# Cross attention on one core: the second score product as two 64-row matmuls instead of two 128-row ones

## The chip, the cores and the metric

The kernel runs on one core of one Trainium2 chip. The metric is device time in microseconds (us). Three runs of the kernel before gave 686.63, 688.91 and 689.27 us; the median is 688.91.

## The reference

For each of 8 batches, with x1 and x2 of shape 512 x 1024 (channels x positions) in float32:

```
q = x1ᵀ Wqᵀ + bq            # 1024 x 64
k = Wk x2 + bk              # 64 x 1024
v = Wv x2 + bv              # 512 x 1024
attn = softmax(q k, axis=2) # 1024 x 1024
out  = v attnᵀ + x1         # 512 x 1024
```

The scores q k contract over 64 rows only. The array of TensorE has 128.

## The kernel before, in words

Every operand of a large product is split into a high part, rounded to the fp32r format, and a low part, the remainder, rounded too. A product is then the sum of three: high·high, high·low, low·high. ScalarE (ACT) makes the high parts by copies, VectorE (DVE) and GpSimd (POOL) make the low parts by subtraction, TensorE (PE) multiplies, and the sync engine (SP) issues all transfers. The order of the work on each engine is written out by hand in one block per engine, and semaphores tie the blocks together.

A batch on PE runs like this (`batch`, L762). The first output half (96 matmuls on `acc_ps`, L731) has the query projection of the next batch (16 matmuls, L670) in its middle. The second output half (96 more) has the key projection of the next batch after its first channel tile and score tiles 0 to 3 of the next batch between its later matmuls. Then `v_phase` (L756) computes the values of the next batch in 8 groups of 12 matmuls (L700), with score tiles 4 to 7 after groups 1, 2, 4 and 5. Seven such batches run in a loop. Batch 0 has a prologue with its own order and the last batch has no successor.

A score tile `scores(t)` (L674) takes 128 queries against all 1024 keys. It fills two banks of `s_ps`, one for each half of the keys, with 512 columns each. Before the change the 128 rows of the stationary operand `q_st` hold the queries' high part in rows 0 to 63 and their low part in rows 64 to 127. The moving operands are `k_hh`, the keys' high part, written twice, once in each half of the partitions, and `k_ll`, the keys' low part, also twice. So a tile is four matmuls of 128 rows and 512 columns: for each key half one with `k_hh` and one with `k_ll`.

These operands come about as follows. PE's projection leaves two partial sums in `s_ps`. ACT copies one of them out (`cross`), DVE joins both with the bias into `full` (`q_sum`, `k_sum`). ACT's `q_high` (L320) copies `full` to the upper rows of `q_st`, and DVE's `q_low` (L467) writes the rest to its lower rows. `k_high` copies twice, `k_low` (L475) subtracts twice over all 1024 columns. `full` is shared by queries and keys.

After a score tile DVE takes the negated row maximum (`neg_max`, L490), ACT the exponential (L337) with the row sum, DVE the reciprocal, the scaling and a transpose in blocks of 32 (`turn`, L506). After four tiles SP issues 16 moves (L208) that put the blocks in place as `pt_raw`. ACT copies `pt_raw` to `pt_hi` and DVE or POOL subtract to `pt_lo` (L455, L271), and these are the moving operands of the output. Between its moves for the second half, SP issues the first load of the next batch's x2, and after them the three others (L184). In ACT's order the rounding of x2's second tile stands before the second `pt_hi` of that half.

Of the kernel before, what the change touches and what calls it, by code (L numbers as in the profile page):

```python
# [36 lines left out]
F32R = mybir.dt.float32r  # L37
# [4 lines left out]
B, C, N, D = 8, 512, 1024, 64  # L42
P = 128
# [3 lines left out]
HALVES = 2  # L47
NH = N // HALVES
# [13 lines left out]
def build(nc, x1_d, x2_d, wq_d, bq_d, wk_d, bk_d, wv_d, bv_d, out_d):  # L62
    with ExitStack() as ctx:
        def sb(name, shape, dt):
            return ctx.enter_context(nc.sbuf_tensor(name, shape, dt))

        def psum(name, shape):
            return ctx.enter_context(nc.psum_tensor(name, shape, F32))

        def sem(name):  # L70
            return ctx.enter_context(nc.semaphore(name))
# [10 lines left out]
        pt_lo = sb("pt_lo", [P, MT, NH], F32R)  # L82
        q_st = sb("q_st", [P, N], F32R)
        k_hh = sb("k_hh", [P, N], F32R)
        k_ll = sb("k_ll", [P, N], F32R)
        cross = sb("cross", [D, N], F32)
        full = sb("full", [D, N], F32)
        o_sb = sb("o_sb", [P, OUTS, NH], F32)
# [21 lines left out]
        s_ps = psum("s_ps", [P, 2, 2, NH])  # L110
# [34 lines left out]
        s_qhi = sem("s_qhi")  # L145
        s_qlo = sem("s_qlo")
        s_khi = sem("s_khi")
        s_klo = sem("s_klo")
# [151 lines left out]
        def _(act):  # L300
            def copy(out, in_):
                return nc.scalar.activation(out, in_, ACT.Copy)  # L302
# [17 lines left out]
            def q_high(b):  # L320
                act.wait_ge(s_qsum, b + 1)
                copy(q_st[0:D, :], full[:]).then_inc(s_qhi, 1)

            def k_cross(b):
                act.wait_ge(s_k, b + 1)
                cross_rows(1).then_inc(s_kcross, 1)
# [43 lines left out]
            def batch(b, last):  # L370
# [6 lines left out]
                if not last:  # L377
                    round_x1(nb, 2)
                    round_x1(nb, 3)
                    q_cross(nb)  # L380
                    round_x2(nb, 0)
                    q_high(nb)
# [45 lines left out]
            q_cross(0)  # L428
            v_hi(0, 2)
            q_high(0)  # L430
            v_hi(0, 3)
            exp(0, 0, first=True)
# [20 lines left out]
        def _(dve):  # L453
            def sub(out, a, hi):
                return nc.vector.tensor_tensor(out, a, hi.bitcast(F32), ALU.subtract)  # L455

            def join(bias, slot):

                return nc.vector.scalar_tensor_tensor(
                    out=full[:], in0=s_ps[0:D, slot, :, :].rearrange("p a n -> p (a n)"), scalar=bias[:, 0:1],  # L460
                    in1=cross[:], op0=ALU.add, op1=ALU.add)

            def q_sum(b):
                dve.wait_ge(s_qcross, b + 1)
                join(bias_q, 0).then_inc(s_qsum, 1)

            def q_low(b):  # L467
                dve.wait_ge(s_qhi, b + 1)
                sub(q_st[D:2 * D, :], full[:], q_st[0:D, :]).then_inc(s_qlo, 1)

            def k_sum(b):
                dve.wait_ge(s_kcross, b + 1)
                join(bias_k, 1).then_inc(s_ksum, 1)

            def k_low(b):  # L475
                for half in range(2):
                    dve.wait_ge(s_khi, b * 2 + half + 1)
                    sub(k_ll[half * D:(half + 1) * D, :], full[:], k_hh[0:D, :]).then_inc(s_klo, 1)

            def low_x1(b, k):  # L480
                dve.wait_ge(s_x1hi, b * KT + k + 1)
                sub(xs_lo[:, k, :], stage[:, k, :], xs_hi[:, k, :]).then_inc(s_x1lo_o, 1)

            def low_x2(b, k):
                dve.wait_ge(s_x2hi, b * KT + k + 1)
                return sub(xs_lo[:, k, :], stage[:, k, :], xs_hi[:, k, :])

            def neg_max(b, t):
                dve.wait_ge(s_s, b * ST + t + 1)
                nc.vector.tensor_reduce(negmax[:, t:t + 1], s_ps[:, t % 2, :, :].rearrange("p a n -> p (a n)"),  # L490
                                        AX_X, ALU.max, negate=True).then_inc(s_max, 1)

            def normalise(b, t):
                dve.wait_ge(s_exp, b * ST + t + 1)
                nc.vector.reciprocal(inv[:, t:t + 1], rowsum[:, t:t + 1]).then_inc(s_inv, 1)
                dve.wait_ge(s_inv, b * ST + t + 1)
                nc.vector.tensor_scalar(probs[:, t % 2, :], probs[:, t % 2, :], inv[:, t:t + 1], None,  # L497
                                        ALU.mult).then_inc(s_norm, 1)

            def turn(b, t, first=False):  # L500

                h, i = t // NT, t % NT
                if i == 0 and not first:
                    dve.wait_ge(s_moved, half_of(b, h) * MOVED - MOVED)
                dve.wait_ge(s_norm, b * ST + t + 1)
                nc.vector.transpose(blocks[:, :, i, :],  # L506
                                    probs[:, t % 2, :].rearrange("p (j r) -> p j r", r=Q)).then_inc(s_blk, 1)

            def v_lo(b, m):
                dve.wait_ge(s_vhi, b * MT + m + 1)  # L510
                sub(vt_lo[:, m, :], acc_ps[:, m % BANKS, :], vt_hi[:, m, :]).then_inc(s_acc, 1)

            def p_lo(b, h, j):

                dve.wait_ge(s_phi, half_of(b, h) * PAIRS + j + 1)
                sub(pt_lo[:, 2 * j:2 * j + 2, :], pt_raw[:, 2 * j:2 * j + 2, :],
                    pt_hi[:, 2 * j:2 * j + 2, :]).then_inc(s_plo, 1)

            def out(b, h, c):

                dve.wait_ge(s_o, b * OG + h * CT + c + 1)
                dve.wait_ge(s_res[c], half_of(b, h) * 16 + 16)
                nc.vector.scalar_tensor_tensor(  # L523
                    out=o_sb[:, c, :], in0=acc_ps[:, c % BANKS, :], scalar=bias_v[:, c:c + 1],
                    in1=o_sb[:, c, :], op0=ALU.add, op1=ALU.add).then_inc(s_acc, 1)
# [23 lines left out]
            def batch(b, last):  # L549
                nb = b + 1  # L550

                dve.wait_ge(s_plo_odd, b * 2 + 2)
                turn(b, 7)
                if not last:
                    low_x1(nb, 1)
                    low_x1(nb, 3)
                out(b, 0, 0)
                out(b, 0, 1)
                if not last:
                    dve.wait_ge(s_klo, nb * 2)  # L560
                    q_sum(nb)
                    q_low(nb)
                out(b, 0, 2)
                for j in range(PAIRS - 1):
                    p_lo(b, 1, j)
                p_lo(b, 1, PAIRS - 1)
                if not last:
                    low_x2(nb, KT - 1).then_inc(s_x2lo_last, 1)
                out(b, 0, 3)

                out(b, 1, 0)
                if not last:
                    dve.wait_ge(s_qlo, nb + 1)
                    k_sum(nb)
                    k_low(nb)
                out(b, 1, 1)
                if last:
                    out(b, 1, 2)
                    out(b, 1, 3)
                    return  # L580
                neg_max(nb, 0)
                normalise(nb, 0)
                neg_max(nb, 1)
                turn(nb, 0)
                out(b, 1, 2)
                normalise(nb, 1)
                neg_max(nb, 2)
                turn(nb, 1)
                normalise(nb, 2)
                neg_max(nb, 3)  # L590
                turn(nb, 2)
                out(b, 1, 3)
                normalise(nb, 3)
                turn(nb, 3)

                v_lo(nb, 0)
                v_phase(nb)
# [25 lines left out]
            q_sum(0)  # L623
            v_lo(0, 2)
            q_low(0)
            v_lo(0, 3)
            neg_max(0, 0)
# [27 lines left out]
            with dve.Fori(0, B - 1) as b:  # L655
                batch(b, False)
# [4 lines left out]
        def _(pe):  # L661
# [10 lines left out]
                return mm  # L672

            def scores(t):  # L674
                rows = q_st[:, t * P:(t + 1) * P]
                for h in range(HALVES):
                    cols = slice(h * NH, (h + 1) * NH)
                    nc.tensor.matmul(s_ps[:, t % 2, h, :], rows, k_hh[:, cols], start=True, stop=False)  # L678
                    mm = nc.tensor.matmul(s_ps[:, t % 2, h, :], rows, k_ll[:, cols], start=False, stop=True)  # L679
                mm.then_inc(s_s, 1)  # L680

            def scores_first(b, t):

                if t == 0:
                    pe.wait_ge(s_qsum, b + 1)
                    pe.wait_ge(s_qlo, b + 1)
                    pe.wait_ge(s_klo, b * 2 + 2)
                else:
                    pe.wait_ge(s_ksum, b + 1)
                scores(t)  # L690
# [185 lines left out]
```

## Time and profile before

| | |
|---|---|
| median of three runs | 688.91 us |
| span of the profiled execution | 687.4 us |
| PE busy | 656.8 us, 96% |
| PE weight loads busy | 534.1 us, 78% |
| DVE busy | 475.1 us, 69% |
| ACT busy | 280.7 us, 41% |
| POOL busy | 139.3 us, 20% |
| matmuls | 2848, of them 256 for the scores |

The profiled execution is known by its span, from its first to its last instruction; a time of its own around the span is not given. Times in the rows are us from the start of the span. A matmul's record lasts longer than the distance to the next matmul's start, because matmuls are pipelined and their ends are modelled. PEld is the weight load that comes before each matmul.

### The profile page before, as it was taken

The page shows a single profiled execution, that of the slowest core. Times are in us where ns is not written, and L with a number is a line of the kernel's source. Part 1 is how long each engine was busy: PE and PEld are TensorE (multiplying, and loading weights), DVE is VectorE, ACT ScalarE, POOL GpSimd, SP SyncE. Part 2 cuts the span into 40 slices and gives each one's busy share as a digit, 9 for nine tenths or more (in the row PEclk, how much of TensorE's full clock was granted, in tenths as well). Part 3 has the DMA queues.
Part 4 walks back from the last instruction along what each step waited for, and adds up shares of the span by engine and source line. Part 5 has one row for each costly group of instructions (what it writes and reads, how often), then busy time and mean ns, then how long its engine had stood idle before and what let it go on. Part 6 is the DMA issues. An engine that isn't in the chain of part 4 may idle for free.

```text
span 687.4 us, 8392 instructions
## 1 busy us (share of the span) xinstructions
PE 656.8 (96%) x2848; PEld 534.1 (78%) x2848; DVE 475.1 (69%) x503; ACT 280.7 (41%) x367; POOL 139.3 (20%) x58
## 2 busy tenths in 40 slices
PE   5999889999999989999899998999989999899997
PEld 3877668887788868888688886888868888788886
DVE  4889558695686765876758866679567695686641
ACT  5564422355235352354423633337232364234220
POOL 0302210063001440032400433005130063101200
PEclk9999989999999999999999999999999999999999
DMA  8400932749328482285624675255941749326351
GB/s 317 187 1 12 265 108 61 193 137 243 102 86 232 116 234 91 84 237 124 197 92 123 197 170 190 75 139 158 229 153 61 174 142 248 107 80 149 73 179 56
DMA packets 94874, 100.04 MB, mean 146 GB/s; under 512 B 8336, under 2 KB 69776, under 8 KB 94864
## 3 DMA queue, kind: packets, MB, share of 16 engines
q1 hardware_dynamic: 94864, 99.91, 51.1%
q8 instruction: 6, 0.10, 0.1%
q14 instruction: 4, 0.03, 0.0%
HBM read 51.64 MB, written 16.78 MB: 100 GB/s over the span
## 4 chain that ended last, share of the span: by engine, by line
PE 81%; DVE 6%; issue 4%; SPq 3%; ACT 3%; DMA 2%; DVEq 0%; ACTq 0%
PE acc_ps L731 39%; PE acc_ps L700 25%; PE s_ps L670 8%; PE s_ps L678 4%; PE s_ps L679 4%; DVE pt_lo L455 4%; SPq L208 3%; DMA stage<-in_ctx_dram 2%; ACT pt_hi L302 2%; ACT xs_hi L302 1%; DVE probs L497 1%; DVE blocks L506 1%; PE s_ps L794 1%; DVE negmax L490 1%; ACT probs L337 0%
## 5 line engine op out<-in xcount | busy, mean ns | idle before, releaser
L731 PE MATMUL acc_ps<-pt_hi,vt_hi 128*128 128x512 f32 x512 | 202.0, 395 | 17.5 <-DVE pt_lo L455 17.5
L731 PE MATMUL acc_ps<-pt_hi,vt_lo 128*128 128x512 f32 x512 | 200.5, 392 | 0.0
L731 PE MATMUL acc_ps<-pt_lo,vt_hi 128*128 128x512 f32 x512 | 200.4, 391 | 0.0
L731 PEld LDWEIGHTS acc_ps<-pt_hi,vt_hi 128*128 128x128 f32 x512 | 96.6, 189 | 44.0 <-DVE pt_lo L455 24.1
L337 ACT ACTIVATE probs<-s_ps,negmax 128x1024 f32<-128x1024 f32 x64 | 71.4, 1116 | 128.4 <-DVE negmax L490 128.4
L271 POOL TENSOR_TENSOR xs_lo<-stage,xs_hi 128x1024 fp32r<-128x1024 f32 x35 | 91.1, 2612 | 156.0 <-ACT xs_hi L302 156.0
L731 PEld LDWEIGHTS acc_ps<-pt_hi,vt_lo 128*128 128x128 f32 x512 | 96.7, 189 | 20.4
L731 PEld LDWEIGHTS acc_ps<-pt_lo,vt_hi 128*128 128x128 f32 x512 | 96.8, 189 | 19.8
L271 POOL TENSOR_TENSOR pt_lo<-pt_raw,pt_hi 128x1024 fp32r<-128x1024 f32 x14 | 41.0, 2946 | 327.5 <-ACT pt_hi L302 327.5
L700 PE MATMUL acc_ps<-wv_hi,xs_hi 128*128 128x512 f32 x256 | 99.9, 390 | 0.0
L700 PE MATMUL acc_ps<-wv_hi,xs_lo 128*128 128x512 f32 x256 | 99.7, 389 | 0.0
L700 PE MATMUL acc_ps<-wv_lo,xs_hi 128*128 128x512 f32 x256 | 99.6, 389 | 0.0
L455 DVE TENSOR_TENSOR pt_lo<-pt_raw,pt_hi 128x1024 fp32r<-128x1024 f32 x46 | 81.8, 1801 | 17.7 <-ACT pt_hi L302 17.4
L490 DVE TENSOR_REDUCE negmax<-s_ps 128x1 f32<-128x1024 f32 x64 | 77.6, 1216 | 11.9 <-PE s_ps L679 11.8
L302 ACT ACTIVATE pt_hi<-pt_raw 128x1024 fp32r<-128x1024 f32 x60 | 60.9, 1049 | 56.8 <-DMA pt_raw<-blocks 35.8
L506 DVE STREAM_TRANSPOSE blocks<-probs 128x1024 f32<-128x1024 f32 x60 | 74.3, 1238 | 6.7 <-DMA pt_raw<-blocks 6.1
L523 DVE SCALAR_TENSOR_TENSOR o_sb<-acc_ps,bias_v,o_sb 128x512 f32<-128x512 f32 x64 | 47.2, 739 | 36.2 <-PE acc_ps L731 35.7
L302 ACT ACTIVATE cross<-s_ps 64x1024 f32<-64x1024 f32 x16 | 16.4, 1025 | 131.5 <-PE s_ps L670 131.5
L455 DVE TENSOR_TENSOR vt_lo<-acc_ps,vt_hi 128x512 fp32r<-128x512 f32 x64 | 43.2, 675 | 35.7 <-ACT vt_hi L302 35.7
L302 ACT ACTIVATE xs_hi<-stage 128x1024 fp32r<-128x1024 f32 x60 | 61.6, 1051 | 10.8 <-DMA stage<-in_ctx_dram 10.7
L700 PEld LDWEIGHTS acc_ps<-wv_lo,xs_hi 128*128 128x128 f32 x256 | 48.2, 188 | 10.0
L700 PEld LDWEIGHTS acc_ps<-wv_hi,xs_hi 128*128 128x128 f32 x256 | 48.2, 188 | 10.0
(49 smaller groups left out, 602.4 us busy)
## 6 DMA issues: line engine op xcount, KB each, us to landing
pt_raw<-blocks SPq DMA_DIRECT2D x240, 128.0 KB, 2.4
stage<-in_ctx_dram SPq DMA_DIRECT2D x32, 512.0 KB, 5.3
o_sb<-in_x_dram SPq DMA_DIRECT2D x64, 256.0 KB, 3.3
out_dram<-o_sb SPq DMA_DIRECT2D x64, 256.0 KB, 2.6
stage<-in_x_dram SPq DMA_DIRECT2D x28, 512.0 KB, 5.9
blocks<-in_x_dram SPq DMA_DIRECT2D x4, 512.0 KB, 8.6
pt_raw<-in_L_xattn_Wv_dram SPq DMA_DIRECT2D x4, 256.0 KB, 8.0
pt_raw<-in_L_xattn_Wk_dram SPq DMA_DIRECT2D x1, 128.0 KB, 3.4
```

The source lines that it names most:

```text
L271: return nc.gpsimd.tensor_tensor(out, src, hi.bitcast(F32), ALU.subtract)
L302: return nc.scalar.activation(out, in_, ACT.Copy)
L337: nc.scalar.activation(probs[:, t % 2, :], s_ps[:, t % 2, :, :].rearrange("p a n -> p (a n)"), ACT.Exp, bias=negmax[:, t:t + 1], accum_out ...
L455: return nc.vector.tensor_tensor(out, a, hi.bitcast(F32), ALU.subtract)
L490: nc.vector.tensor_reduce(negmax[:, t:t + 1], s_ps[:, t % 2, :, :].rearrange("p a n -> p (a n)"), AX_X, ALU.max, negate=True).then_inc(s_m ...
L506: nc.vector.transpose(blocks[:, :, i, :], probs[:, t % 2, :].rearrange("p (j r) -> p j r", r=Q)).then_inc(s_blk, 1)
L523: nc.vector.scalar_tensor_tensor(out=o_sb[:, c, :], in0=acc_ps[:, c % BANKS, :], scalar=bias_v[:, c:c + 1], in1=o_sb[:, c, :], op0=ALU.add ...
L670: mm = nc.tensor.matmul(s_ps[:, slot, h, :], weights[:, k, :], cols, start=(k == 0 and part == 0), stop=(k == KT - 1 and part == 1))
L678: nc.tensor.matmul(s_ps[:, t % 2, h, :], rows, k_hh[:, cols], start=True, stop=False)
L679: mm = nc.tensor.matmul(s_ps[:, t % 2, h, :], rows, k_ll[:, cols], start=False, stop=True)
L700: mm = nc.tensor.matmul(acc_ps[:, m % BANKS, :], x[:, k, cols], w[:, k, :], start=(k == 0 and w is wv_hi and x is xs_hi), stop=(k == KT - ...
L731: mm = nc.tensor.matmul(acc_ps[:, c % BANKS, :], v[:, m, cols], p[:, m, :], start=(m == 0 and v is vt_hi and p is pt_hi), stop=(m == MT - ...
```

## The change

In place of `k_ll` there are two buffers. `k_lo` holds the low part of the first key half in partitions 0 to 63 and of the second key half in partitions 64 to 127. `q_dup` holds a second copy of the queries' high part in partitions 64 to 127. A score tile is now two 128-row matmuls with `k_hh` as before, and then two matmuls of 64 rows: `q_st`'s upper rows times the first half of `k_lo` into the first bank, and `q_dup`'s rows times the second half of `k_lo` into the second bank. The product of the two low parts, which the 128-row form added as well, is left out. ACT makes one more copy per batch, DVE subtracts half as many columns, and three waits are added or moved.

```diff
-        k_ll = sb("k_ll", [P, N], F32R)
+        q_dup = sb("q_dup", [P, N], F32R)
+        k_lo = sb("k_lo", [P, NH], F32R)
...
                 copy(q_st[0:D, :], full[:]).then_inc(s_qhi, 1)
+                copy(q_dup[D:2 * D, :], full[:]).then_inc(s_qhi, 1)
...
             def q_low(b):
-                dve.wait_ge(s_qhi, b + 1)
+                dve.wait_ge(s_qhi, b * 2 + 1)
...
             def k_low(b):
-                for half in range(2):
-                    dve.wait_ge(s_khi, b * 2 + half + 1)
-                    sub(k_ll[half * D:(half + 1) * D, :], full[:], k_hh[0:D, :]).then_inc(s_klo, 1)
+                for h in range(HALVES):
+                    dve.wait_ge(s_khi, b * 2 + h + 1)
+                    cols = slice(h * NH, (h + 1) * NH)
+                    sub(k_lo[h * D:(h + 1) * D, :], full[:, cols], k_hh[0:D, cols]).then_inc(s_klo, 1)
...
                     dve.wait_ge(s_qlo, nb + 1)
+                    dve.wait_ge(s_qhi, nb * 2 + 2)
                     k_sum(nb)
...
             def scores(t):
-                rows = q_st[:, t * P:(t + 1) * P]
+                rows = slice(t * P, (t + 1) * P)
                 for h in range(HALVES):
-                    cols = slice(h * NH, (h + 1) * NH)
-                    nc.tensor.matmul(s_ps[:, t % 2, h, :], rows, k_hh[:, cols], start=True, stop=False)
-                    mm = nc.tensor.matmul(s_ps[:, t % 2, h, :], rows, k_ll[:, cols], start=False, stop=True)
+                    nc.tensor.matmul(s_ps[:, t % 2, h, :], q_st[:, rows], k_hh[:, h * NH:(h + 1) * NH],
+                                     start=True, stop=False)
+                for h, q_hi in enumerate((q_st[0:D, rows], q_dup[D:2 * D, rows])):
+                    mm = nc.tensor.matmul(s_ps[:, t % 2, h, :], q_hi, k_lo[h * D:(h + 1) * D, :],
+                                          start=False, stop=True)
                 mm.then_inc(s_s, 1)
...
                     pe.wait_ge(s_qlo, b + 1)
+                    pe.wait_ge(s_qhi, b * 2 + 2)
                     pe.wait_ge(s_klo, b * 2 + 2)
```

## Rows read from the trace of the kernel before

**Rows 1.** The page, part 1: busy us (share of the span) xinstructions.

```profile
PE 656.8 (96%) x2848; PEld 534.1 (78%) x2848; DVE 475.1 (69%) x503; ACT 280.7 (41%) x367; POOL 139.3 (20%) x58
```

**Rows 2.** The page, part 4: the chain that ended last, by engine.

```profile
PE 81%; DVE 6%; issue 4%; SPq 3%; ACT 3%; DMA 2%; DVEq 0%; ACTq 0%
```

**Rows 3.** Windows of two batches: us, busy of each engine, granted clock, DMA.

```profile
core 0: us, PE busy (x) PEld busy (x) DVE busy (x) ACT busy (x) POOL busy (x), PEclk, DMA share, GB/s
...
174.57:258.04 83.47, 80.55 (x352) 65.94 (x353) 58.79 (x63) 34.54 (x45) 18.82 (x7) 1.00 0.54 151
...
340.59:423.12 82.53, 80.52 (x353) 65.92 (x353) 58.87 (x63) 34.44 (x45) 18.89 (x7) 1.00 0.54 153
```

**Rows 4.** Timeline of PE around one score tile: start us, us, engine, line, operation.

```profile
194.45 0.39 PE L678 MATMUL s_ps<-k_hh,q_st 128*128 128x512 f32 x1
...
195.35 0.39 PE L731 MATMUL acc_ps<-pt_hi,vt_hi 128*128 128x512 f32 x1
```

**Rows 5.** Timeline of PE and its weight loads just after a stall.

```profile
174.57 0.19 PEld L731 LDWEIGHTS acc_ps<-pt_hi,vt_hi 128*128 128x128 f32 x1 [2.10 <-DVE pt_lo L455]
174.57 0.50 PE L731 MATMUL acc_ps<-pt_hi,vt_hi 128*128 128x512 f32 x1 [1.67 <-DVE pt_lo L455]
174.68 0.19 PEld L731 LDWEIGHTS acc_ps<-pt_lo,vt_hi 128*128 128x128 f32 x1
...
174.91 0.40 PE L731 MATMUL acc_ps<-pt_lo,vt_hi 128*128 128x512 f32 x1
```

**Rows 6.** Timeline of weight loads in the prologue: eight in a row.

```profile
45.06 0.86 PEld L794 LDWEIGHTS s_ps<-ident,probs 128*128 128x128 f32 x8 [0.45 <-DVE probs L497]
```

**Rows 7.** Groups by line and form: count, busy us, mean ns of one, idle before.

```profile
L679 PE MATMUL s_ps<-k_ll,q_st 128*128 128x512 f32 x128 | 49.9, 390 | 0.0
...
L455 DVE TENSOR_TENSOR k_ll<-full,k_hh 64x1024 fp32r<-64x1024 f32 x16 | 19.5, 1218 | 8.1 <-ACT k_hh L302 7.9
...
L302 ACT ACTIVATE q_st<-full 64x1024 fp32r<-64x1024 f32 x8 | 8.4, 1056 | 2.9 <-DVE full L459 2.9
```

**Rows 8.** Timeline of ACT from the queries' copy to the second output half.

```profile
161.03 1.06 ACT L302 ACTIVATE q_st<-full 64x1024 fp32r<-64x1024 f32 x1 [0.39 <-DVE full L459]
165.51 1.06 ACT L302 ACTIVATE pt_hi<-pt_raw 128x1024 fp32r<-128x1024 f32 x1 [3.41 <-PE acc_ps L731]
```

**Rows 9.** Timeline of ACT and DVE in the prologue.

```profile
29.32 1.06 ACT L302 ACTIVATE q_st<-full 64x1024 fp32r<-64x1024 f32 x1 [0.90 <-DVE full L459]
...
30.55 0.60 ACT L302 ACTIVATE vt_hi<-acc_ps 128x512 fp32r<-128x512 f32 x1 [0.16 <-PE acc_ps L700]
...
32.94 1.23 DVE L490 TENSOR_REDUCE negmax<-s_ps 128x1 f32<-128x1024 f32 x1 [0.58 <-PE s_ps L679]
```

**Rows 10.** Timeline of DVE from the first score tile to the last turn.

```profile
189.66 1.23 DVE L490 TENSOR_REDUCE negmax<-s_ps 128x1 f32<-128x1024 f32 x1 [1.60 <-PE s_ps L679]
...
204.14 1.25 DVE L506 STREAM_TRANSPOSE blocks<-probs 128x1024 f32<-128x1024 f32 x1
...
230.23 0.16 DVE L495 RECIPROCAL inv<-rowsum 128x1 f32<-128x1 f32 x1 [0.37 <-ACT probs L337]
```

**Rows 11.** Timeline of SP's queue: moves and x2 loads.

```profile
205.41 10.53 SPq L208 DMA_DIRECT2D pt_raw<-blocks  x16
...
244.34 1.70 SPq L184 DMA_DIRECT2D stage<-in_ctx_dram  x3
...
327.65 1.74 SPq L184 DMA_DIRECT2D stage<-in_ctx_dram  x3
```

**Rows 12.** Timeline of ACT where it uses moved and loaded data.

```profile
217.89 2.01 ACT L302 ACTIVATE pt_hi<-pt_raw 128x1024 fp32r<-128x1024 f32 x2 [2.56 <-DMA pt_raw<-blocks]
...
250.03 1.06 ACT L302 ACTIVATE xs_hi<-stage 128x1024 fp32r<-128x1024 f32 x1 [0.90 <-DMA stage<-in_ctx_dram]
...
332.50 1.04 ACT L302 ACTIVATE xs_hi<-stage 128x1024 fp32r<-128x1024 f32 x1
```

**Rows 13.** Window of the first loop batch with the lower clock.

```profile
87.40:95.10 7.70, 6.71 (x18) 4.80 (x17) 5.53 (x4) 0.46 (x1) 1.51 (x1) 0.56 0.45 147
```

## The prediction

> **What bounds the kernel now.** I read the profile in this order. First the busy table: PE is busy 96% of the 687.4 us span, DVE 69% [rows 1]. Then the chain of waits: PE holds 81% of it [rows 2]. Then the windows by batch, cut at the point where PE leaves its stall: an undisturbed batch lasts 82.53 us, 80.52 of it PE, so PE idles 2.0 us per batch [rows 3]. All of that idleness sits at the start of the second output half, where PE waits for DVE's pt_lo; elsewhere the loop's matmuls follow each other without a gap. Then the timeline around one score tile: matmul starts at 194.45 and, four later, at 195.35 [rows 4], a pitch of 0.227 us (0.90 / 4). So 8 score tiles of 4 matmuls cost PE 7.3 us per batch, and every one of them stands on PE's own time.
>
> What a weight load costs shows only after a stall [rows 5]. The load starts at 174.57 and its matmul record is 0.50 us long instead of 0.39; the next load starts at 174.68 and the next matmul at 174.91. So a load occupies the array 0.11 us, the next load begins when the matmul before it starts to stream, and it is hidden under the 0.23 us of streaming. Eight loads in a row took 0.86 us [rows 6], again 0.11 each.
>
> **The change on PE.** A score tile was four 128-row matmuls (64 tiles, 256 matmuls, half of them on k_ll [rows 7]). It becomes two 128-row matmuls and then two 64-row ones on different rows of the array and different PSUM banks. The instruction count is the same, so the gain exists only if the last two stream side by side. The trace of before has no 64-row matmul, so I bound the pair's time P against today's 2 x 0.227 = 0.454:
> - Lower bound: both loads (2 x 0.11 = 0.22) hide under the matmul ahead, and both stream together, P = 0.227, a saving of 0.227 per tile.
> - By the order in rows 5, one load ahead at a time: the second load starts when the first 64-row matmul streams, so the second starts 0.11 later, P = 0.34, a saving of 0.117.
> - Serial: P = 0.454, saving 0.
> - Upper bound: going from 128-row to 64-row work and back empties the array. A matmul's record is 0.389 against a pitch of 0.227, so waiting for its end costs 0.162, twice per tile 0.324; if the loads come out from cover too, 2 x 0.11 more. Net 0.10 (with the full saving) to 0.43 dearer per tile.
>
> I take 0.117, because rows 5 are the nearest to it: they show when a load is let go.
>
> Two rules of the Trainium skill pull apart here. "TensorE: Matmul & The Clock Gate", the part on packing small matmuls, says that loads for other row groups are pulled ahead and that packed matmuls start some 4 ns apart: that would be the lower bound, 64 x 0.227 = 14.5 us of PE work. "TensorEngine Tiling (Array Packing)", Key Properties, says that changing the tiling mode, not merely the tile, drains the engine; this kernel changes it twice in each tile, which would be the upper bound. No run so far shows either.
>
> **The change on ACT and DVE.** ACT gains one 64x1024 copy (q_dup) per batch: 1.06 us, as q_st's [rows 7]. In the loop it comes after the copy at 161.03 and before pt_hi at 165.51, ahead of which ACT sits idle 3.41 us [rows 8]: hidden, with 2.3 us to spare. Without that cover it would be 1.06 x 7 = 7 us. DVE's q_low waits for the first copy only. PE's new wait for the second copy comes some 25 us later in the loop. In the prologue it does not hide fully: q_st ends at 30.38, q_dup would end at 31.4, and v_hi (30.55 before), and v_lo on DVE behind it, slip so that the first neg_max (32.94 [rows 9]) starts up to 0.3 us later. k_low goes from 2 x 1.22 to about 2 x 0.65 us (half the columns and a little; my estimate): DVE is 1.1 us less busy, but DVE then waits 1.60 us for PE before neg_max [rows 10], so it gives nothing. The extra DVE wait before k_sum was met long before.
>
> **What is late next.** PE's saving is worth its full size only while the other chain follows. From the first score tile of a batch, DVE and ACT run a chain of their own [rows 10]: neg_max at 189.66, dense work to the turn at 204.14; then 16 moves take SP 10.53 us [rows 11]; ACT waits 2.56 us for them at 217.89 [rows 12]; DVE is dense again and idles only 0.37 before the last reciprocal. Then come 16 moves more, the three x2 loads, the copy xs_hi and behind it pt_hi. These loads have little slack: issued at 327.65, used at 332.50 (4.85 us) in a good batch; issued at 244.34, used only at 250.03 with 0.90 us of waiting in the one bad batch, and that batch lasted 83.47 instead of 82.5 [rows 3, 11, 12]. So per batch the first tile's saving is free, and of the other seven tiles' saving only 0.37 us plus the loads' slack (0 to about 0.8, I take 0.4) gets through.
>
> **Sum.** With 0.117 per tile, the seven tiles bring PE 0.82 us of lead, of which 0.37 + 0.4 = 0.77 count; with the first tile 0.89 us per batch, times 7 batches = 6.2. The prologue's 8 tiles give 0.94 less 0.3 for q_dup, 0.6; but one load in seven that lands late takes some 0.6 back. Total 6.2 us: span 687.4 to 681.2. The span of the profiled execution is 1.5 below the median of the runs (688.91), and what lies around it does not change: 682.7 us. With the lower bound the seven tiles lead by 1.59 and again 0.77 get through: (0.23 + 0.77) x 7 + 1.5 = 8.5 us, 680.4; with the loads' slack at 0.8 it would be 677. With 0.117 and no slack in the loads: (0.117 + 0.37) x 7 + 0.6 = 4.0, 684.9. The answer is thus nearly the same for both ways of overlapping: 677 to 685.
>
> **Rivals.**
> 1. Serial pair. The two 64-row matmuls go through one after the other, or overlap and lose it again in switching. For it: rows 4 show matmuls strictly one by one, at one pitch whatever the operands. Against it: the two use disjoint rows and other banks. Time: 688.9, with 0.3 for the prologue 687.5 to 690.
> 2. Mode change empties the array (the slower side). Place: between the second 128-row matmul and the first 64-row one, and again behind the pair, in each of 64 tiles, all on PE's own time. Price 0.324 for the tails. It decides as soon as it exceeds the saving, that is from 0.06 to 0.11 us per switch. With the full saving 0.10 x 64 = 6.2, 695; with the staggered one 0.21 x 64 = 13.2, 702; with exposed loads as well 0.42 x 64 = 27, 716. For it: 128 switches, each with the other kind of work directly behind. Against it: nothing in this trace switches row sizes, and the switch from 128-column transposes to ordinary matmuls keeps its 0.11 us load pitch. The Trainium skill's tiling page, named above, is the rule by which it would come out so.
> 3. The lead turns into a stall that lowers the clock. PE's wait at the second half grows by up to 0.8 us. In the first batch three such waits brought the granted clock to 0.56, near the 1.2 GHz level, over 87.4 to 95.1 us [rows 13]: 17 matmuls at 0.43, 3.4 us lost. In seven batches that would be 24 us. Against it: the bad batch with a 0.94 longer stall kept a clock of 1.00 [rows 3]. I give it little.
>
> **Chances.** Overlap, either kind: 0.45 (677 to 685). Serial or evened out: 0.20. Emptying array: 0.33, of which 695 to 702 holds 0.19 and 716 holds 0.14. Lower clock: 0.02. Time 682.7, range 677 to 702: left out are 716, the clock case and a little below 677. The likeliest case alone has 677 to 685. A difference under 0.5% (3.4 us) can't be told from none here; 0.45 faster, 0.20 same, 0.35 slower.
>
> **What would show it.** In the timeline of a score tile: the two k_lo matmuls start 0.11 us apart (my step), some ns apart (lower bound) or 0.23 apart (serial), and four starts of a tile plus the next matmul span 0.79 us instead of 0.90; over 1.0 would be the emptying array, seen as a longer gap at either switch. In the windows: PE's records per batch unchanged in number, the batch at 81.6 us instead of 82.5, and PE's idle before pt_lo not smaller than 2.0. In the waits: more ACT waiting for the x2 stage loads. ACT's q_dup copy has no waiter in the loop. The prediction is wrong if the pair isn't nearer to 0.34 than to 0.454, or if the stall at the second half eats more than the 0.1 us per batch that I allow.

## The result: 1.6% slower, and the profile after

The changed kernel takes 698.96 us (median of 4 runs, 697.80 to 700.16), against 688.71 us for the kernel before. The ratio is 1.0156, with a 95% interval of 1.0132 to 1.0179. Ratios and intervals here and below use fast runs alone, that is without those more than 1.5% above the fastest of their kernel, of which only e1c has any. The forecast was 682.7 us, 0.9% faster; the time lies between the 695 and 702 us of rival 2, the array that empties when the row size changes. The profiled execution took 697.8 us, with a span of 696.0 us.

The page of the kernel after, part 1 and part 4, answers to [rows 1] and [rows 2]:

```profile
PE 665.2 (96%) x2848; PEld 515.1 (74%) x2848; DVE 466.6 (67%) x503; ACT 290.1 (42%) x375; POOL 139.6 (20%) x58
...
PE 81%; DVE 6%; issue 4%; SPq 3%; ACT 3%; DMA 2%; DVEq 0%; ACTq 0%
```

The bound is the same as before, PE. It has the same 2848 matmuls and is busy 8.4 us longer. DVE has 8.5 us less to do and ACT 9.4 us more; experiment e3 shows that ACT's part costs nothing.

The window of one undisturbed loop batch of the kernel after answers to [rows 3]; its columns are the same:

```profile
174.34:258.49 84.15, 82.14 (x353) 63.80 (x353) 57.97 (x63) 35.67 (x46) 18.96 (x7) 1.00 0.53 150
```

A batch takes 84.15 instead of 82.53 us. That is 1.62 us for 8 score tiles, 0.20 per tile, all of it PE's busy time (82.14 against 80.52). PE's idle time is still 2.0 us.

Where the 0.20 lies shows in the timeline of PE and its weight loads around one score tile of the kernel after, which answers to [rows 4] (start us, us, engine, line, operation, rows*columns of the array):

```profile
194.59 0.61 PE L681 MATMUL s_ps<-k_hh,q_st 128*128 128x512 f32 x2
195.13 0.18 PEld L684 LDWEIGHTS s_ps<-k_lo,q_st 64*128 64x128 f32 x1 [0.35 <-issue]
195.13 0.50 PE L684 MATMUL s_ps<-k_lo,q_st 64*128 64x512 f32 x1
195.13 0.18 PEld L684 LDWEIGHTS s_ps<-k_lo,q_dup 64*128 64x128 f32 x1
195.14 0.50 PE L684 MATMUL s_ps<-k_lo,q_dup 64*128 64x512 f32 x1
195.56 0.19 PEld L738 LDWEIGHTS acc_ps<-pt_hi,vt_hi 128*128 128x128 f32 x1 [0.24 <-issue]
195.56 0.50 PE L738 MATMUL acc_ps<-pt_hi,vt_hi 128*128 128x512 f32 x1
195.67 0.19 PEld L738 LDWEIGHTS acc_ps<-pt_lo,vt_hi 128*128 128x128 f32 x1
195.90 0.39 PE L738 MATMUL acc_ps<-pt_lo,vt_hi 128*128 128x512 f32 x1
```

Read it with the clue of [rows 5]: a record of 0.50 instead of 0.39 us has waited for its own load. The two 64-row matmuls start 0.01 us apart, and their two loads together: the overlap is complete. But the loads are not under the matmul ahead. The second 128-row matmul streams from 194.82 to 195.05 (two times 0.227 from 194.59). The loads start only at 195.13, 0.08 later, and the streaming another 0.11 later. The way back is the same: the pair streams from 195.24 to 195.47, the next load starts at 195.56, 0.09 later, and its matmul streams from 195.67. Each change of row size thus costs a gap of 0.08 to 0.09 and a load of 0.11 out of cover. "Issue" as releaser says that no semaphore held the load. That the array is empty in the gap is not shown: the record of the second 128-row matmul, whose end is modelled, runs to 195.20 and so beyond the start of the load.

From one tile's first start to the streaming of the matmul behind it there are 1.08 us (195.67 less 194.59), where before there were 0.90 [rows 4]. The next six or so matmuls keep a pitch of 0.23 instead of 0.227, which adds some 0.03. So the overlap gives back 0.227 per tile and the two changes take 0.43.

The sum over the kernel: from 174.34 to the same point five batches later, 595.11, are 420.77 us; before, from 174.57 to 588.15, 413.58. The difference of 7.2 is 5 x 1.62 less the 0.94 of the late batch that this execution of before had [rows 3]. The first eight tiles show no cost in this pair of executions: PE leaves its last wait of the first batch at 90.11 us, and before at 90.06, because the first batch waits for loads. (That instant moves by itself: in e3, whose score tiles are those of before, it is 90.75.) The 56 tiles after that make 11.4 us. The profiled execution of before had its late batch (0.94) and, from the lower clock of [rows 13], a first loop batch of 84.51 us instead of 82.53 on top, so the spans differ by 8.6 only.

### The profile page after: what moved, and what is told of

The parts are those of the page before. It is cut to its first block, busy times and chain, and to the rows that moved or that the text cites. A ratio compares the mean times of both kernels' runs of the same rounds, so it can differ in the third digit from the quotient of the medians.

```text
span 696.0 us, 8408 instructions
## 1 busy us (share of the span) xinstructions
PE 665.2 (96%) x2848; PEld 515.1 (74%) x2848; DVE 466.6 (67%) x503; ACT 290.1 (42%) x375; POOL 139.6 (20%) x58
## 4 chain that ended last, share of the span: by engine, by line
PE 81%; DVE 6%; issue 4%; SPq 3%; ACT 3%; DMA 2%; DVEq 0%; ACTq 0%
PE acc_ps L738 39%; PE acc_ps L707 26%; PE s_ps L674 8%; PE s_ps L681 4%; PE s_ps L684 4%; DVE pt_lo L457 4%; SPq L209 3%; DMA stage<-in_ctx_dram 2%; ACT pt_hi L303 1%; ACT xs_hi L303 1%; DVE probs L500 1%; DVE blocks L509 1%; DVE negmax L493 0%; PE s_ps L801 0%; ACT probs L339 0%
## 5 line engine op out<-in xcount | busy, mean ns | idle before, releaser
L738 PE MATMUL acc_ps<-pt_hi,vt_hi 128*128 128x512 f32 x512 | 204.2, 399 | 18.1 <-DVE pt_lo L457 18.1
L707 PE MATMUL acc_ps<-wv_hi,xs_hi 128*128 128x512 f32 x256 | 103.4, 404 | 0.0
L303 ACT ACTIVATE vt_hi<-acc_ps 128x512 fp32r<-128x512 f32 x64 | 38.0, 594 | 58.3 <-PE acc_ps L707 57.1
```

What stands on the lines that cost most here:

```text
L707: mm = nc.tensor.matmul(acc_ps[:, m % BANKS, :], x[:, k, cols], w[:, k, :], start=(k == 0 and w is wv_hi and x is xs_hi), stop=(k == KT - ...
L738: mm = nc.tensor.matmul(acc_ps[:, c % BANKS, :], v[:, m, cols], p[:, m, :], start=(m == 0 and v is vt_hi and p is pt_hi), stop=(m == MT - ...
```

## The experiments

Each ran beside the kernel before on the same chip, in three series: e1, e2, e8 and e4 (before at 687.50 us), e3, e5 and e1c (688.47), and the last three (688.61). Times of different series compare to about a microsecond. "Undisturbed batch" is the distance between the ends of PE's wait in two consecutive batches where no load was late. In that measure before has 82.53 us and the changed kernel 84.15. "Per tile" is an eighth of a difference in it.

**e1: three 128-row matmuls per tile.** What would PE's full saving have brought?

```diff
-                    nc.tensor.matmul(s_ps[:, t % 2, h, :], rows, k_hh[:, cols], start=True, stop=False)
-                    mm = nc.tensor.matmul(s_ps[:, t % 2, h, :], rows, k_ll[:, cols], start=False, stop=True)
+                    mm = nc.tensor.matmul(s_ps[:, t % 2, h, :], rows, k_hh[:, cols], start=True, stop=h == 1)
+                    if h == 0:
+                        nc.tensor.matmul(s_ps[:, t % 2, h, :], rows, k_ll[:, cols], start=False, stop=True)
```

> The kernel before with three instead of four 128-row matmuls in each score tile: the low product of the second key half is left out. PE's own time falls by 0.227 us per tile, which is the most that a perfectly overlapped pair could have saved, with no 64-row work at all. Theory of the prediction (the chain of DVE, the moves and the x2 loads lets only about 1.0 us per batch through): 680 us, and ACT waits for the x2 stage loads in most batches. Rival (that chain has more slack than I read, everything passes): 64 x 0.227 = 14.5 us less, 674 us, 1.82 us less per batch.

Measured: 683.22 us (680.45 to 687.24, 12 runs), ratio 0.9942, interval 0.9920 to 0.9964. So of 14.5 us only about 4 arrive. The windows of e1 show a batch (columns as in [rows 3]):

```profile
418.77:499.88 81.11, 78.99 (x344) 64.35 (x344) 59.08 (x63) 34.51 (x45) 18.95 (x7) 1.00 0.54 154
```

1.4 of the 1.82 us get through in such a batch, more than my 1.0 and less than all. That batches save this much and the whole kernel only 4 us has two reasons in sight: the first batch gains nothing (PE leaves its last wait at 90.23 us), and the runs of e1 range over 7 us where those of before beside it range over 4. Part of the loss per batch is not where I looked for it. It is seen on PE and on DVE in the timeline of e1, in the first output half:

```profile
391.98 0.64 DVE L455 TENSOR_TENSOR vt_lo<-acc_ps,vt_hi 128x512 fp32r<-128x512 f32 x1
...
392.10 0.39 PE L732 MATMUL acc_ps<-pt_hi,vt_lo 128*128 128x512 f32 x1
392.68 0.50 PE L732 MATMUL acc_ps<-pt_hi,vt_hi 128*128 128x512 f32 x1 [0.20 <-DVE vt_lo L455]
```

PE reaches the last chunk of the first output tile before DVE has made the last v_lo (`vt_lo` in the rows): 0.58 between two starts instead of 0.227. The idle time in brackets understates it, since a record outlasts its pitch. The place that I named shows too: in two of the five batches, 81.46 and 81.98 us long, PE's first wait at the second half is 0.61 and 1.19 us instead of 0.33, with ACT late by a wait for the x2 load.

**e2: both 64-row matmuls on the same rows.** `k_lo` becomes 64 partitions of 1024 columns, and both matmuls read `q_st`'s upper rows.

```diff
-                for h, q_hi in enumerate((q_st[0:D, rows], q_dup[D:2 * D, rows])):
-                    mm = nc.tensor.matmul(s_ps[:, t % 2, h, :], q_hi, k_lo[h * D:(h + 1) * D, :],
+                for h in range(HALVES):
+                    mm = nc.tensor.matmul(s_ps[:, t % 2, h, :], q_st[0:D, rows], k_lo[:, h * NH:(h + 1) * NH],
```

> The changed kernel with both 64-row matmuls on array rows 0 to 63 (q_st's upper rows, k_lo as 64 partitions of 1024 columns), so that they can't run side by side. Theory M (every change between 128-row and 64-row work costs about 0.2 us, and the pair's overlap gives 0.227 back): the overlap goes, the switches stay, 64 x 0.227 = 14.5 us over the changed kernel, 713.5 us; the second 64-row matmul starts 0.23 behind the first with its load hidden. Rival L (the gaps come from loading two row groups at once): the gaps vanish, 689 us or little more.

Measured: 712.62 us (4 runs), ratio 1.0377 (1.0355 to 1.0399). A window of e2, and a tile in its timeline of PE:

```profile
177.72:263.72 86.00, 83.96 (x352) 64.64 (x352) 58.09 (x63) 35.79 (x46) 19.51 (x7) 1.00 0.53 146
```

```profile
198.45 0.61 PE L681 MATMUL s_ps<-k_hh,q_st 128*128 128x512 f32 x2
198.99 0.73 PE L684 MATMUL s_ps<-k_lo,q_st 64*128 64x512 f32 x2
199.65 0.50 PE L738 MATMUL acc_ps<-pt_hi,vt_hi 128*128 128x512 f32 x1
```

Batches are 0.43 per tile over before and 0.23 over the changed kernel. The overlap is worth its full 0.227, and the rest of the price stays, with the second 64-row load hidden: two records of 0.50 and 0.39 make 0.73 together when their streaming is 0.23 apart. Loading two row groups is not the cause.

**e8: one 64-row matmul per tile.**

```diff
-                for h in range(HALVES):
+                for h in (1, 0):
                     nc.tensor.matmul(s_ps[:, t % 2, h, :], q_st[:, rows], k_hh[:, h * NH:(h + 1) * NH],
-                                     start=True, stop=False)
-                for h, q_hi in enumerate((q_st[0:D, rows], q_dup[D:2 * D, rows])):
-                    mm = nc.tensor.matmul(s_ps[:, t % 2, h, :], q_hi, k_lo[h * D:(h + 1) * D, :],
-                                          start=False, stop=True)
+                                     start=True, stop=h == 1)
+                mm = nc.tensor.matmul(s_ps[:, t % 2, 0, :], q_st[0:D, rows], k_lo[0:D, :],
+                                      start=False, stop=True)
```

> The changed kernel with only one 64-row matmul in each tile, that of the first key half; the low product of the second key half is left out. Theory M: the second 64-row matmul was free and the switches cost the same, so 699 us as the changed kernel, and 25 us over the run that leaves out the same product with 128-row matmuls if nothing caps that one. Rival L (two row groups' loads make the gaps): 0.11 to 0.2 us per tile less, 686 to 692 us.

Measured: 696.15 us (694.82 to 698.66), ratio 1.0131 (1.0108 to 1.0153). The window of an undisturbed batch:

```profile
257.29:341.20 83.91, 81.91 (x344) 63.77 (x344) 57.82 (x63) 35.56 (x46) 18.88 (x7) 1.00 0.53 150
```

That is 0.2 less than with the pair. So the second 64-row matmul is nearly free, 0.03 per tile. One single 64-row matmul among 128-row ones costs almost all of the loss: compared with e1, which leaves out the same product, it is 13 us slower. The 25 us expected were for an e1 that nothing caps.

**e4: 128, 64, 128, 64 rows.**

```diff
-                for h in range(HALVES):
+                for h, q_hi in enumerate((q_st[0:D, rows], q_dup[D:2 * D, rows])):
                     nc.tensor.matmul(s_ps[:, t % 2, h, :], q_st[:, rows], k_hh[:, h * NH:(h + 1) * NH],
                                      start=True, stop=False)
-                for h, q_hi in enumerate((q_st[0:D, rows], q_dup[D:2 * D, rows])):
```

> The changed kernel with the four matmuls of a tile in the order 128, 64, 128, 64 rows: four changes of row size per tile instead of two and no overlap of the 64-row ones. Theory M: four times 0.2 us on top of the 0.907 of before, 64 x 0.8 = 51 us over the kernel before, 740 us. Rival D (only the return to 128 rows, or only the first entry into a tile, costs): 0.4 us per tile less, 714 us.

Measured: 740.26 us (4 runs), ratio 1.0768 (1.0752 to 1.0784), 52.8 us over before; batches of 89.4 us, 0.86 per tile, 0.21 per change. The timeline of PE in e4 shows that the ways in and out cost the same:

```profile
201.58 0.40 PE L681 MATMUL s_ps<-k_hh,q_st 128*128 128x512 f32 x1
201.91 0.50 PE L683 MATMUL s_ps<-k_lo,q_st 64*128 64x512 f32 x1
202.34 0.50 PE L681 MATMUL s_ps<-k_hh,q_st 128*128 128x512 f32 x1
202.77 0.50 PE L683 MATMUL s_ps<-k_lo,q_dup 64*128 64x512 f32 x1
203.19 0.50 PE L737 MATMUL acc_ps<-pt_hi,vt_hi 128*128 128x512 f32 x1
203.53 0.39 PE L737 MATMUL acc_ps<-pt_lo,vt_hi 128*128 128x512 f32 x1
```

The starts are 0.43, 0.43 and 0.42 apart, where 0.227 is the pitch without a change. (The first distance, 0.33, is shorter and the last, 0.34, too: only a record of 0.50 begins with its load, 0.11 before it streams. Counted from streaming to streaming the first is 0.44 and the last 0.23.)

**e3: ACT's copy and the waits alone.**

```diff
+        q_dup = sb("q_dup", [P, N], F32R)
...
                 copy(q_st[0:D, :], full[:]).then_inc(s_qhi, 1)
+                copy(q_dup[D:2 * D, :], full[:]).then_inc(s_qhi, 1)
...
-                dve.wait_ge(s_qhi, b + 1)
+                dve.wait_ge(s_qhi, b * 2 + 1)
...
+                    dve.wait_ge(s_qhi, nb * 2 + 2)
...
+                    pe.wait_ge(s_qhi, b * 2 + 2)
```

> The kernel before with the change's edits on ACT and the waits alone: the second copy q_dup and the waits for it, while the scores stay four 128-row matmuls on k_ll and DVE's subtractions stay as they were. Theory M (all of the loss is on PE at the switches): no difference beyond the measurement, 687.5 us within 1 us. Rival A (the copy delays ACT somewhere on the path, 1.06 us per batch): up to 7 us more, 694 us.

Measured: 687.31 us (12 runs), ratio 0.9992 (0.9974 to 1.0010), and undisturbed batches of 82.54 us. The side edits cost nothing. DVE's shorter subtraction was not run by itself; it takes work away from an engine that waits for PE.

**e5: two tiles share one change.**

```diff
+            def both(t):
+                scores_hi(t)
+                scores_hi(t + 1)
+                scores_lo(t)
+                scores_lo(t + 1)
...
-                    if m in (1, 2, 4, 5):
-                        scores_next(b, NT + (1, 2, 4, 5).index(m))
+                    if m in (1, 4):
+                        both_next(b, NT + 2 * (m // 4))
...
```

> The changed kernel with tiles 0 and 1, 4 and 5, 6 and 7 taken together: four 128-row matmuls of both tiles, then both pairs of 64-row ones; tiles 2 and 3 of the loop stay single, the prologue has four groups. Theory M: one entry and one exit serve two pairs, a group costs 4 x 0.227 + 2 x 0.227 + 0.43 = 1.79 us against 1.81 for two old tiles and 2.21 for two single changed ones. Per batch 2 x 0.2 from the single tiles less 3 x 0.02, so 0.34 us over the kernel before, 690 us in all, 9 us under the changed kernel. Rival S (each pair pays its own 0.4, since it is the 64-row loads that can't be covered): as the changed kernel, 699 us. Rival T (the grouping itself delays the first row maximum and the chain behind it): 693 to 695 us.

The timeline of PE in e5 around one group (`scores_hi` is L681, `scores_lo` L687):

```profile
191.20 1.07 PE L681 MATMUL s_ps<-k_hh,q_st 128*128 128x512 f32 x4
192.20 0.49 PE L687 MATMUL s_ps<-k_lo,q_st 64*128 64x512 f32 x1
192.20 0.49 PE L687 MATMUL s_ps<-k_lo,q_dup 64*128 64x512 f32 x1
192.53 0.39 PE L687 MATMUL s_ps<-k_lo,q_st 64*128 64x512 f32 x1
192.54 0.39 PE L687 MATMUL s_ps<-k_lo,q_dup 64*128 64x512 f32 x1
192.86 0.50 PE L753 MATMUL acc_ps<-pt_hi,vt_hi 128*128 128x512 f32 x1
```

The second pair has records of 0.39 us: within 64-row work the loads hide again. Two pairs pay one way in and one way out, and the group takes 1.77 us (192.97 less 191.20) against 1.81 for two old tiles. The windows of e5 show an undisturbed batch and a disturbed one:

```profile
177.23:260.13 82.90, 80.91 (x352) 63.79 (x352) 57.84 (x63) 35.59 (x46) 18.87 (x7) 1.00 0.54 152
260.13:343.84 83.71, 80.91 (x353) 63.80 (x353) 57.86 (x63) 35.69 (x46) 18.83 (x7) 1.00 0.54 150
```

82.90 is 0.37 over before, as theory M said (0.34). The whole took 694.11 us (692.41 to 695.99), ratio 1.0078 (1.0052 to 1.0103), 4 us more than theory M expected and inside rival T's 693 to 695. The trace bears rival T out, in the prologue: PE stands still in front of the second, third and fourth group for 1.13, 1.08 and 2.31 us. The last of these is the first row below (e5); the second row is the last single tile of the changed kernel's prologue, the only one there with such a wait.

```profile
56.41 1.19 PE L681 MATMUL s_ps<-k_hh,q_st 128*128 128x512 f32 x4 [2.31 <-ACT probs L339]
...
53.32 0.73 PE L681 MATMUL s_ps<-k_hh,q_st 128*128 128x512 f32 x2 [0.78 <-ACT probs L339]
```

By its edit the last group waits until both score slots have been read, where a single tile waits for one. PE leaves its last wait of the first batch at 94.33 us, 4.2 later than in the changed kernel. Two batches of the loop are late besides, by 0.8 and 1.4 us, with ACT waiting 0.77 and 1.44 us for an x2 load. Why those loads are later is not settled.

**e1c: v_lo earlier in DVE's order**, on top of e1.

```diff
+                v_lo(b, 7)
                 neg_max(b, 7)
                 turn(b, 6)
-                v_lo(b, 7)
                 normalise(b, 7)
```

> The run with three instead of four 128-row matmuls per tile (the low product of the second key half left out), and in addition DVE makes v_lo of the last group before the last neg_max and the turn before it instead of after them. Theory C (of the 1.82 us that PE saves per batch about 0.45 is lost because PE reaches the last chunk of the first output tile before DVE's v_lo of group 7): that wait of 0.35 us goes, batches take 80.7 instead of 81.15 us, 3 us less over the loop, 680 us. Rival X (the x2 loads, moved 1.1 us later relative to nothing else, cap it in its stead): the same 81.1 us per batch, with the wait moved to the start of the second output half, 683 us.

Measured: 685.04 us (679.73 to 694.93, 12 runs), ratio 0.9937 (0.9907 to 0.9968), no gain over e1. Rival X holds: with that wait gone, another takes its place, and the batches take 81.2 to 81.9 us. A window of e1c, and its PE and ACT in the timeline at the start of a second half:

```profile
416.56:498.25 81.69, 78.73 (x344) 64.41 (x345) 59.22 (x63) 34.49 (x45) 18.80 (x7) 1.00 0.56 154
```

```profile
488.53 1.06 ACT L302 ACTIVATE pt_hi<-pt_raw 128x1024 fp32r<-128x1024 f32 x1 [2.85 <-DMA pt_raw<-blocks]
490.24 1.07 ACT L302 ACTIVATE xs_hi<-stage 128x1024 fp32r<-128x1024 f32 x1 [0.65 <-DMA stage<-in_ctx_dram]
...
494.93 0.50 PE L732 MATMUL acc_ps<-pt_hi,vt_hi 128*128 128x512 f32 x1 [1.31 <-DVE pt_lo L455]
```

PE's first wait there grows from 0.33 to 1.31 us. Of the 0.98 more, 0.65 is ACT's wait for the x2 load. The rest lies ahead of it: this pt_hi waits for the moves, where before it waited for PE [rows 8]; in this trace it does so in three of the six loop batches after the first. So the moves and the loads arrive at the limit together.

Ten of the 12 runs lie between 679.73 and 688.75 us, and roughly in step with the mean granted clock: four at 0.997 or more took 679.7 to 680.6 us, five at 0.992 or less 683.4 to 688.8. That PE's waits are what lowers the clock in them is not shown by this trace, which has 1.00 throughout; e1cl below is the run with rows on it.

**e5l, bl, e1cl: the x2 load before the last four moves.**

```diff
-                move(b, 1, range(2, NQ))
+                move(b, 1, range(2, 3))
+                if not last:
+                    next_x2(nb, 1)
+                move(b, 1, range(3, NQ))
                 if not last:
-                    for k in range(1, KT):
+                    for k in range(2, KT):
```

> The grouped kernel (tiles 0 and 1, 4 and 5, 6 and 7 together) with one edit on SP: the second of the next batch's four x2 loads is issued before the last four moves of the second half instead of behind them. Theory D (the grouped kernel's undisturbed batches are at 82.9 us, and its loss above 690 us comes from batches in which ACT waits for that load, 0.8 and 1.4 us in two of them, and from the first batch): ACT no longer waits for the load, all loop batches at 82.9 us, 690 to 692 us. Rival G (the grouping's own delay of the first row maximum): unchanged, 694 us.

> The kernel before with the same edit on SP alone. Theory D: its one late batch (83.47 instead of 82.53 us) and the stalls of the first batch shrink, 686 to 687.5 us, that is up to 2 us less and hardly to be told from none. Rival (the last moves land later by the load's 512 KB and pt_hi waits for them): 689 us or more.

> The run with three 128-row matmuls per tile (low product of the second key half left out) and v_lo early, with the same edit on SP. Theory D (with v_lo out of the way the x2 loads alone cap the gain): PE's wait at the second half falls back from 1.05 to 1.5 us to 0.33 in its first part, batches take 80.7 us instead of 81.7, and the granted clock stays at 1.00; 677 to 679 us. Rival (the moves, issued over 10.5 us by SP, are the cap and not the load behind them): batches stay at 81.5 us or more, 683 us.

Measured: 704.55, 701.66 and 698.13 us, ratios 1.0225 (1.0207 to 1.0243), 1.0154 (1.0116 to 1.0193) and 1.0148 (1.0127 to 1.0169). All three lose 10 to 13 us against the kernel that they were made from, and theory D holds in none. The repair was wrong, and bl's rival is the one that came about. SP's queue and ACT in the timeline of bl:

```profile
244.35 0.85 SPq L184 DMA_DIRECT2D stage<-in_ctx_dram  x1
245.24 2.58 SPq L208 DMA_DIRECT2D pt_raw<-blocks  x4
...
253.19 1.06 ACT L305 ACTIVATE pt_hi<-pt_raw 128x1024 fp32r<-128x1024 f32 x1 [5.40 <-DMA pt_raw<-blocks]
```

The last four moves are issued from 245.24 to 247.82, and ACT can use them only at 253.19. From issue to landing they take 4.8 to 5.9 us. The same four take 3.1 to 3.6 us in the kernel before, where one load less stands ahead of them, and a move with no load ahead of it takes 2.4 in both. So the second load of 512 KB costs each of them 1.2 to 2.7 us of landing, on top of a later issue. The five batches behind the first two have a third wait on PE and last 84.4 to 84.9 us. So these three runs say nothing on whether the x2 loads alone cap e1 or delay e5; that stays open.

In e1cl the clock adds to the loss, against its theory D: all five runs have a mean granted clock of 0.975 to 0.985. Two windows of it:

```profile
176.73:259.25 82.52, 79.18 (x344) 64.50 (x344) 59.25 (x63) 34.40 (x45) 18.86 (x7) 1.00 0.54 153
...
337.50:344.40 6.90, 5.84 (x12) 3.66 (x12) 6.23 (x3) 5.04 (x6) 5.79 (x2) 0.51 0.38 122
```

Behind the first batch there are four such stretches at the 1.2 GHz level. Each begins in, or within 0.8 us behind, a wait of PE of 1.9 to 3.2 us at the second half, and the batches that hold one take 84.2 to 85.6 us, where the first row has 82.52 at full clock. So rival 3 is real for a PE that is ahead. The length of the wait does not decide it alone: the changed kernel's first batch has a wait of 2.75 us, and its clock stays at 1.00.

## Why the prediction was wrong, point by point

- *What bounds the kernel.* Right: PE, with 0.227 us per matmul, and a loss on PE's own time passed through in full (1.62 us per batch).
- *A load takes 0.11 us.* Right. Uncovered, it is the larger half of the price of each change, beside a gap of 0.08 to 0.09.
- *The pair's time P.* This step failed. I took 0.34, because [rows 5] show one load let go at a time, and so let the second matmul start 0.11 late. It starts 0.01 late, since both loads start at the same time (195.13). But the size of P was not what decided: e2 and e5 show 0.227 per pair, the lower bound, and the kernel is slower all the same. What failed is that I carried the cover of loads, which [rows 5] show among 128-row matmuls, over to a place where the row size changes, and gave the changes no price in the value I took. They cost 0.43 per tile, and the saving of 0.117 became a loss of 0.20.
- *The upper bound.* The mechanism of rival 2 was right, at the place named, twice per tile. Its terms were off. I put the emptying at 0.162 per change, from the length of a record; the gap is 0.08 to 0.09. I counted the loads' exposure in the dearest version alone; it is there at every change. My middle version, 702 us, has 0.21 per tile and the measured net is 0.20. That they are so close is luck, for the terms are others: full overlap, a shorter gap, exposed loads.
- *Against rival 2* I held that the switch from transposes to ordinary matmuls keeps the load pitch. Those are 128-row instructions too. It was evidence on another kind of change, and none on this one. The Trainium skill's rule (TensorEngine Tiling (Array Packing), Key Properties: a change of tiling mode drains the engine, a change of tile doesn't) agrees with all of e2, e4, e5 and e8, in that the gap of 0.08 to 0.09 us stands at every change of row size and at no change of tile; whether the engine is drained in it no run shows. What the Trainium skill's page "TensorE: Matmul & The Clock Gate" says of packed matmuls starting almost together, in its part on packing small matmuls, agrees with the 0.00 to 0.01 us between the starts of a pair. The two did not pull apart: one is about matmuls within a mode, the other about the border.
- *ACT and DVE.* Right on ACT: e3 shows no difference. q_dup lies in ACT's idle time, which falls from 3.41 to 2.33 us ahead of pt_hi.
- *What is late next.* Right in kind, and off in size both ways: with the full saving an undisturbed batch of e1 gains 1.4 of 1.82 us, where I said 1.0, but the kernel gains 4 us, where I said 8.5. The first cap is DVE's last v_lo, whose slack of 1.3 us (made by 313.24 in the kernel before, needed at 314.63) I had left out of the sum; e1c shows a second one right behind, at the moves and the x2 loads.
- *The sum.* It took 1.5 us from the profiled span to the time, by setting the span beside the median of other runs. In each execution on record the two are about 1.8 us apart, so the same sum would give 683.0.
- *The lower clock.* It played no part in the loss: the changed kernel's profiled execution has a clock of 1.00. Its price was too high: of the 3.4 us that I counted for the stretch in [rows 13], 2.0 reach the batch (84.51 against 82.53), since part of it falls where PE would have waited anyway.
- *The chances.* 0.33 for the emptying array was too little, given that a rule spoke for it and no row against it.
- *The signs.* A longer gap at either switch was the right thing to look for; from the first start of a tile to the streaming behind it there are 1.08 us, over the 1.0 named. The two signs of being wrong looked elsewhere: the pair, at 0.23, is nearer to 0.34 than to 0.454, and the stall at the second half is still 2.0 us. Neither watches the borders of the pair, where the time went.

## What to carry to other kernels

Halving the rows of a matmul, with the two halves on different rows of the array, doubles the rate only inside a run of such matmuls. Each way in and each way out costs about one full matmul here (0.21 us against 0.227), so a pair between 128-row work loses 0.20, two pairs in a row break even (1.77 against 1.81 us), and by these figures a gain needs three or more behind one another. That is an estimate and was not run; the kernel's two score slots in PSUM don't allow it. Before counting a saving on the bound engine, read how far the next chain lies behind: one matmul less per tile brought little more than a quarter of its nominal worth. Grouping work on the bound engine has a price of its own where the group must wait for all that its parts wait for (4.2 us in the prologue of e5). And a large load put between small transfers that someone waits for delays these, even if it is itself the one that is late.

## What the runs showed of the hardware

- Two 64-row matmuls on different halves of the array, with fp32r operands and different banks, stream fully side by side: starts 0.00 to 0.01 us apart, 0.227 us for both.
- A change between 128 and 64 rows costs 0.20 to 0.21 us in either direction: a gap of 0.08 to 0.09 after the last streaming, then the weight load of 0.11 uncovered.
- A single 64-row matmul between 128-row ones costs as much as a pair (0.03 us less per tile).
- Four moves issued behind two loads of 512 KB landed 4.8 to 5.9 us after issue (bl), behind one 3.1 to 3.6, and with none ahead 2.4 (before).
- Where PE waited 1.9 to 3.2 us at the second half, the granted clock fell to the 1.2 GHz level in four loop batches of e1cl; waits of 2.75 us in the changed kernel's trace and of 3.56 us in that of e5 left it at 1.00.
